# Broadcast of the softmax reciprocals issued one query block later, and the zero point of the int weights taken off by column sums instead of on the weights

## The reference

```
xn   = layernorm(x) * ln_scale + ln_bias
xg   = concat([16 global tokens, xn])                    # T = 2048 tokens + G = 16
Q, K, V = xg @ Wq.T, xg @ Wk.T, xg @ Wv.T                # 16 heads of 128
S    = Q K^T / sqrt(128) + mask                          # band of 256 keys, and the 16 global keys
attn = softmax(S) @ V
x1   = layernorm(x + (attn @ Wo.T + x))
gate = silu(x1 @ ((wq_gate - 128) * s_gate[:, None]).T)  # wq_* are int32 in 0..255, 5632 x 2048
up   = x1 @ ((wq_up - 128) * s_up[:, None]).T
y    = (gate * up) @ ((wq_down - 128) * s_down[:, None]).T
out  = layernorm(x1 + y)
```

## Time and profile before

| | us |
|---|---|
| median of 3 runs (lowest, highest) | 5631.65 (5619.04, 5742.77) |
| the profiled execution, its time | 5661.84 |
| its span on the slowest core, core 7 | 5660.3 |
| spans of the eight cores | 5595.5 to 5660.3 |
| PE busy | 3669.3 (65%) |
| DVE busy | 1381.9 (24%) |
| ACT busy | 930.2 (16%) |

### The profile page before, as it was taken

How to read it: one execution, slowest core, us unless ns; L and a number is a source line. 1 busy time by engine, 2 the same in 40 slices (tenths; PEclk the granted TensorE clock), 3 DMA queues, 4 the chain that set the end, 5 groups by cost and what they waited for, 6 DMA issues and landing times.

```text
span 5660.3 us, 46164 instructions; the slowest of 8 cores (5595.5 to 5660.3 us)
## 1 busy us (share of the span) xinstructions
PE 3669.3 (65%) x15128; PEld 1440.1 (25%) x15128; DVE 1381.9 (24%) x2076; ACT 930.2 (16%) x1175; POOL 302.8 (5%) x577
## 2 busy tenths in 40 slices
PE   2386686777677656170799985555129999755550
PEld 1132231232222112030344432222004444322220
DVE  6523323333322321324222210000241222000003
ACT  0001101111111110000233331111003333211110
POOL 0000000000000000000000001111000000111110
PEclk9977778888788778685799999998659999999895
DMA  2200100110110116433344433333334444233323
GB/s 81 67 10 14 35 11 13 28 19 13 29 19 8 17 30 117 134 89 144 80 75 76 80 56 51 40 50 62 98 126 78 75 75 75 45 52 52 62 34 150
DMA packets 210620, 335.31 MB, mean 59 GB/s; under 512 B 112452, under 2 KB 157509, under 8 KB 196565
## 3 DMA queue, kind: packets, MB, share of 16 engines
q0 software_dynamic: 82400, 180.46, 20.0%
q1 hardware_dynamic: 127990, 151.90, 8.2%
HBM read 458.20 MB, written 54.53 MB: 91 GB/s over the span
## 4 chain that ended last, share of the span: by engine, by line
PE 56%; DMA 17%; DVE 15%; issue 7%; ACT 3%; DVEq 1%; ACTq 0%; another core or an unknown queue 0%; SPq 0%; POOLq 0%; POOL 0%
PE p_gu L914 21%; DMA wdTt<-wd 9%; PE p_sc L452 5%; PE p_sc L500 4%; PE p_sc L464 4%; PE p_wo L699 4%; DVE rowBt L586 4%; PE p_gu L1024 4%; PE p_sc L546 2%; DVE statst L292 2%; DMA xrest<-x 2%; ACT wdTt L1006 2%; DMA r2tt<-r2sp 2%; PE p_srow L1162 2%; PE p_sc L549 2%
## 5 line engine op out<-in xcount | busy, mean ns | idle before, releaser
L1024 PE MATMUL p_gu<-wdTt,hmidt 128*128 128x512 bf16 x1408 | 401.8, 409 | 529.5 <-ACT wdTt L1006 501.0
L914 PE MATMUL p_gu<-xn2ht,wgTt 128*128 128x512 bf16 x2816 | 639.7, 380 | 31.1 <-ACT wuTt L890 28.8
L914 PE MATMUL p_gu<-xn2ht,wuTt 128*128 128x512 bf16 x2816 | 636.5, 379 | 0.0
L565 ACT ACTIVATE p_sbt<-p_sc 128x512 bf16<-128x512 f32 x352 | 208.8, 598 | 1446.0 <-PE p_sc L549 1446.0
L1006 ACT ACTIVATE wdTt<-wdTt 128x512 bf16<-128x512 bf16 x352 | 222.2, 631 | 1059.2 <-DMA wdTt<-wd 985.2
L699 PE MATMUL p_wo<-woTt,aott 128*128 128x512 bf16 x1024 | 229.1, 388 | 218.2 <-DMA aott<-aosp 177.5
L914 PEld LDWEIGHTS p_gu<-xn2ht,wgTt 128*128 128x128 bf16 x2816 | 275.4, 98 | 367.8 <-issue 40.7
L914 PEld LDWEIGHTS p_gu<-xn2ht,wuTt 128*128 128x128 bf16 x2816 | 275.5, 98 | 332.3
L1024 PEld LDWEIGHTS p_gu<-wdTt,hmidt 128*128 128x128 bf16 x1408 | 123.7, 101 | 784.7 <-issue 706.4
L883 ACT ACTIVATE wgTt<-wgTt 128x2048 bf16<-128x2048 bf16 x88 | 168.2, 1912 | 848.2 <-DMA wuTt<-wu 848.2
L600 PE MATMUL p_rbc<-rowHt,ones_rowt 1*128 1x512 bf16 x64 | 37.1, 580 | 408.1 <-DVE rowLt L593 408.1
(11 more groups left out here) (96 smaller groups left out, 3191.7 us busy)
## 6 DMA issues: line engine op xcount, KB each, us to landing
wgTt<-wg POOLq DMA_DIRECT2D x88, 512.0 KB, 5.1
wuTt<-wu POOLq DMA_DIRECT2D x88, 512.0 KB, 7.1
wdTt<-wd POOLq DMA_DIRECT2D x352, 128.0 KB, 2.9
r2tt<-r2sp SPq DMA_DIRECT2D x32, 1024.0 KB, 6.5
xtilet<-x SPq DMA_DIRECT2D x16, 1024.0 KB, 5.5
aott<-aosp SPq DMA_DIRECT2D x32, 512.0 KB, 4.2
woTt<-wo POOLq DMA_DIRECT2D x8, 2048.0 KB, 31.2
xrest<-x SPq DMA_DIRECT2D x16, 1024.0 KB, 6.9
```

The source lines that it names most:

```text
L565: return act.activation(p_sb[:, (i % 4) * 512:(i % 4 + 1) * 512], bank.p[:, :], AF.Exp)
L914: ins = t.matmul(bank.p[:, :], wsl[:, j * D + dc * 128:j * D + (dc + 1) * 128], xn2h[:, dc * 1024 + tc * 512:dc * 1024 + (tc + 1) * 512], ...
L1024: ins = t.matmul(pd_banks[ti].p[:, :], hmid[:, hb * 1024 + ti * 128:hb * 1024 + (ti + 1) * 128], wdT[:, j * 512:(j + 1) * 512], start=(hb ...
```

## The change

Two independent edits.

First, the tail of a query block is cut in two. The DVE row chain (`rowA` to `rowL`) stays where it was. The rest (the two matmuls L600 and L602, the copy L611, the multiply L619 and SP's store) is put into a list and written out only after the next block's last P V matmul, ahead of that block's own DVE row chain. The tail of a head's last block so comes after the first block of the next head, behind that head's Q and K matmuls.

Second, ACT no longer adds -128 to the weights: PE waits for the DMA itself. In its place PE sums `xn2h` over the contraction at the start of each pass (2 x 16 matmuls with one output row, into the one bank `b_cs`), DVE splits the row into `rowH` and `rowL`, and every bank of gate and up gets two more matmuls of 512 columns with one contraction row (`neg128` times `rowH`, `rowL`). Before down, `hmid` is summed in the same manner (2 x 44 matmuls), and after the 44th weight tile every one of the 8 banks gets two more matmuls, with `rowH` or `rowL` stationary and `neg128` moving. With this, PE waits for all 8 banks to be free before the first matmul of a column block; before, each matmul waited for its own bank.

The diff, cut to its core:

```diff
@@ attention, at the end of the P V matmuls of a block
                     emit_pv(h, q4, nk - 1, klist, hh, t_exp, t_pvmm, t_pv)
                     t_pv[(h, q4)] = s_pe.tok
+                    while pending_tail:
+                        pending_tail.pop(0)()
...
                     blk.vector(f)
                     t_rhl4 = s_dve.tok
-                    def f(t, h=h, q4=q4, t_rhl4=t_rhl4):
-                        wt(t, t_rhl4)
...
+                    def tail_fin(h=h, q4=q4, t_rhl4=t_rhl4):
+                        def f(t):
+                            wt(t, t_rhl4)
+                            wt(t, b_rb.freed)
+                            t.matmul(b_rb.p[:, :], ones_row[:, :], rowH[:, q4 * 512:(q4 + 1) * 512],
+                                     start=True, stop=False)
+                            ins = t.matmul(b_rb.p[:, :], ones_row[:, :], rowL[:, q4 * 512:(q4 + 1) * 512],
+                                           start=False, stop=True)
...
+                    pending_tail.append(tail_fin)
+
+        while pending_tail:
+            pending_tail.pop(0)()
         barrier()
@@ feed-forward, at the start of a pass
-            t_cshl = t_xn2
+            t_csev = {}
+            for tc in range(2):
+                def f(t, p=p, tc=tc, t_xn2=t_xn2):
+                    wt(t, t_xn2)
...
+                    wt(t, b_cs.freed)
+                    for dc in range(ND):
+                        ins = t.matmul(b_cs.p[0:1, :], ones_col[:, :],
+                                       xn2h[:, dc * 1024 + tc * 512:dc * 1024 + (tc + 1) * 512],
+                                       start=(dc == 0), stop=(dc == ND - 1))
...
@@ loads of gate and up
-                def fs(act, hb=hb, j=j, wgT=wgT, _t_ld=_t_ld, _t_pw=_t_pw,
...
-                    return act.activation(wgT[:, j * D:(j + 1) * D], wgT[:, j * D:(j + 1) * D],
-                                          AF.Copy, bias=-128.0)
...
+                t_wgld[hb] = s_wg[j].tok
@@ matmuls of gate and up
                             for dc in range(ND):
-                                ins = t.matmul(bank.p[:, :],
...
+                            t.matmul(bank.p[:, :], neg128[:, 0:128],
+                                     rowH[:, tc * 512:(tc + 1) * 512], start=False, stop=False)
+                            ins = t.matmul(bank.p[:, :], neg128[:, 0:128],
+                                           rowL[:, tc * 512:(tc + 1) * 512], start=False, stop=True)
@@ between gate/up and down
-            t_hcshl = t_hmid_all
+            for tc in range(2):
+                def f(t, p=p, tc=tc, t_hmid_all=t_hmid_all):
+                    wt(t, t_hmid_all)
+                    wt(t, b_cs.freed)
+                    for hb in range(NHB):
+                        ins = t.matmul(b_cs.p[0:1, :], ones_col[:, :],
...
@@ down
                         if hb == 0:
                             wt(t, t_hcshl)
+                            for ti in range(8):
+                                wt(t, pd_banks[ti].freed)
                         for ti in range(8):
-                            if hb == 0:
-                                wt(t, pd_banks[ti].freed)
...
                         if hb == NHB - 1:
                             for ti in range(8):
-                                pd_banks[ti].used = (s_pe, s_pe.n)
+                                t.matmul(pd_banks[ti].p[:, :],
+                                         rowH[:, ti * 128:(ti + 1) * 128], neg128[:, :],
+                                         start=False, stop=False)
+                                ins = t.matmul(pd_banks[ti].p[:, :],
+                                               rowL[:, ti * 128:(ti + 1) * 128], neg128[:, :],
+                                               start=False, stop=True)
+                                pd_banks[ti].used = s_pe.inc(ins)
```

More of the change, by code:

```diff
@@ L959, in build_nc, with f @@
             pxs.close()
-            t_hcshl = t_hmid_all
+            t_hcs_ev = {}
+            for tc in range(2):
+                def f(t, p=p, tc=tc, t_hmid_all=t_hmid_all):
+                    wt(t, t_hmid_all)
+                    wt(t, b_cs.freed)
+                    for hb in range(NHB):
+                        ins = t.matmul(b_cs.p[0:1, :], ones_col[:, :],
+                                       hmid[:, hb * 1024 + tc * 512:hb * 1024 + (tc + 1) * 512],
+                                       start=(hb == 0), stop=(hb == NHB - 1))
+                    b_cs.used = s_pe.inc(ins)
+                blk.tensor(f)
+                def f(dve, p=p, tc=tc):
+                    wt(dve, b_cs.used)
+                    dve.wait_ge(s_dve.h, s_dve.n)
+                    b_cs.freed = s_dve.inc(dve.tensor_copy(rowA[:, tc * 512:(tc + 1) * 512],
+                                                           b_cs.p[0:1, :]))
+                blk.vector(f)
+                t_hcs_ev[tc] = s_dve.tok
+            def f(dve, p=p):
+                wt(dve, t_hcs_ev[1])
+                dve.wait_ge(s_dve.h, s_dve.n)
+                s_dve.inc(dve.tensor_copy(rowH[:, 0:1024], rowA[:, 0:1024]))
+                dve.wait_ge(s_dve.h, s_dve.n)
+                s_dve.inc(dve.tensor_tensor(rowC[:, 0:1024], rowA[:, 0:1024],
+                                            rowH[:, 0:1024], ALU.subtract))
+                dve.wait_ge(s_dve.h, s_dve.n)
+                s_dve.inc(dve.tensor_copy(rowL[:, 0:1024], rowC[:, 0:1024]))
+            blk.vector(f)
+            t_hcshl = s_dve.tok
             b_s2 = [Bank(psa(p4p, "p_s20_%d" % p, [128, 512])),
@@ L1015, in build_nc, with f @@
                     j = hb % 2
+                    def f(pool, p=p, e4=e4, hb=hb, j=j):
+                        prev = t_dpe.get((p, e4, hb - 2)) or t_dpe.get((p, e4 - 1, NHB - 2 + hb)) \
+                            or t_dpe.get((p - 1, 3, NHB - 2 + hb))
+                        wt(pool, prev)
+                        if e4 == 0 and hb < 2:
+                            wt(pool, t_gu[(p, NHB - 1)])
+                            wt(pool, t_hmid[(p, NHB - 1, 1)])
+                            if p > 0:
+                                wt(pool, t_outst[(p - 1, 7)])
+                        s_wd[j].inc(pool.dma_start(out=wdT[:, j * 512:(j + 1) * 512],
+                                                   in_=wd_in[e4, hb * 128:(hb + 1) * 128, :]), 16)
+                    blk.gpsimd(f)
+                    t_wdld[(e4, hb)] = s_wd[j].tok
                     def f(t, p=p, e4=e4, hb=hb, j=j):
```

161 lines of the change are left out of this document (57 added, 104 removed).

## The result

The changed kernel is faster: the ratio of its time to that of the kernel before is 0.9412, 95% interval 0.9373 to 0.9451. The forecast was 5290 us, 0.939 of the time before. In most executions of either kernel the cores of one or both dies were granted a lower clock and the time was longer, so the ratios and the single times in this document are of executions without that (for the changed kernel 5287.04, 5300.87 and 5314.54 us, the first of them profiled). The median over eight executions of every kind is 5528.9 us (5287.04 to 5776.14); that of the kernel before is 5743.41 over ten, not the 5631.65 of the first three. The forecast was for a median, and 5528.9 lies above its range of 5190 to 5400 us.

What follows compares the result with a forecast made beforehand. PE was taken to bound the kernel, with large waits in down (501.0 us) and attention (408.1 us). Terms -496 + 215 + 4 + 40 - 129 + 21 = -345 from the 5631.65 median gave 5290 us, range 5190 to 5400.

Steps and rivals of the forecast that it cites:

- The sum of -345: Whole kernel: all forecast terms added, -496 + 215 + 4 + 40 - 129 + 21 = -345 us.
- Attention, -496: Attention: deferring the two matmuls saves 31.0 us a head over 16 heads, -496 us.
- t0: Attention: start of a block's last row-sum matmul (L1157 before); next first P V forecast 3.74 us later, 9.81 before.
- 6.33: Attention: forecast time in us from a full block's first P V to its last row sum.
- rival A: Attention gives back half: clock stays low between 1.2 us stalls, or unseen DVE step; time 5540 to 5630; chance 0.05.
- 17.53: Attention: time in us of a full block before the change; forecast 10.07 after.
- The wait at P V: Attention: new PE wait for DVE's `rowA` at a block's first P V, about 1.2 us, some 48 times.
- Gate and up, +215: Gate and up: 704 added matmuls cost 152 us, switches between 128 contraction rows and one 63 more.
- Rival B: Gate and up: one-row matmuls cost far more than 0.09 us a switch; kernel slower from 0.58; chance 0.02.
- Start of down, +20 a pass: Before down: sums of `hmid`, row work and waiting take 26.6 us instead of 6.47 idle; +40 in all.
- Down, -129 + 21: Down: load's turn 5.76 us instead of 6.53, -129 us; column-block transitions +20 and last blocks +1.
- Rival C: Dense stages: granted clock falls to 0.81 after the change, costing 300 us; time 5590; chance 0.03.

## Why the prediction was right and wrong

- **The time itself.** The failed step is "the forecast is for a median, so 5631.65 - 345". The median of three executions was taken for that of the kernel, and nothing was set down for its moving with more of them. Over ten it is 5743.41, and the changed kernel's over eight is 5528.9: outside the range, and 214 us below the one before, not 345. The sum of -345 itself fits the two profiled executions (5631.7 and 5285.5 us on core 0, 346 apart), and its 0.939 the measured 0.9412. But it fits by luck: two of its terms were wrong by about 100 us in opposite directions.
- **Attention, -496: right in mechanism, 95 us too large.** The first P V came at t0 + 3.63 against 3.74 worked out, the end of a head took 0.84 us instead of 1.05, `rowL` was ready, and `wqkT` never late. The step that failed is "6.33", the time from the first P V to the last row sum, taken from a stretch at full clock. PE stops for `rowA` in 47 of the 48 full blocks of core 0. After 39 of these stops the matmuls went on at half clock and it was 7.6 to 9.1 us; after the other 8 it was 6.32, the forecast's own number within 0.01. Three of the 8 are those of head 12, of which this is the first:

```profile
1399.31 0.37 PE L1173 MATMUL p_srow<-p_gt,ones_colt 16*1 16x512 bf16 x1
...
1402.94 0.38 PE L1176 MATMUL p_pv<-p_sbt,v4t 128*128 128x512 bf16 x1 [1.76 <-DVE rowAt L583]
...
1409.27 0.37 PE L1173 MATMUL p_srow<-p_gt,ones_colt 16*1 16x512 bf16 x1
```

   The mean block is 11.41 us and not 10.07, 64 us over the 48. The forecast had this as rival A and gave it 0.05 on the ground that PE in down stops for 2.85 us and still runs at full clock. That one turn was not the rule. In the same trace, on core 7, 24 of the 97 stops over 2.5 us in down are followed by matmuls at half clock; the earlier trace rows shows it after a longer one (4 matmuls in 1.87), and so does this one of the usual length:

```profile
3386.14 1.86 PE L1024 MATMUL p_gu<-wdTt,hmidt 128*128 128x512 bf16 x4 [2.83 <-ACT wdTt L1006]
```

   The experiment with the tail further forward shows that with a stop of 0.67 us in its place the half clock is gone. A second, smaller part: the 17.53 us a block before came from head 2 of core 7; the mean of the 48 on core 0 is 17.11, so 20 us of the gain were never there to be had.
- **The wait at P V was called 1.2 us and was 1.76.** The forecast took the difference of the two paths, 3.74 less 2.54; but PE stands idle from the end of the second score pair on, also while the exp that either path waits for is made. It was the stop and not the difference that had to be held against the clock.
- **Gate and up, +215: right.** 352 x (4.09 - 3.46) = 222 us, and the bounds and the choice of the row L1160 to L1162 for the switch held. Rival B (0.58 us a switch) is excluded by the 0.10 and 0.09 measured.
- **Start of down, +20 a pass: right.** 27.5 us against some 6.9 before.
- **Down, -129 + 21: 106 us too small a gain.** The failed step is the turn: "the load's turn loses ACT's 0.77". Over the eight column blocks of core 0, each from the end of its first weight tile to the end of its 44th (21.5 turns), the turns took 1194.3 us before and 972.2 after, 6.94 and 5.65 us each. A turn lost 1.29 us and not 0.77, 222 us in all and not 129. The 5.65 is close to the forecast's 5.76; it is the turn before that was read too short, from one of 6.53 in the earlier trace rows. Of the 222 us, 174 are PE's stops before a weight tile (478.1 to 304.3), and 51 are matmuls that no longer run at half clock: the eight matmuls of a tile took longer than the 1.51 us of full clock in 62 of 344 tiles before and in 24 after. The turn in the earlier trace rows had none of these. Why the stops alone shrank by 1.0 us a turn, and not by 0.77, is not shown. The transitions were nearly right: the six of core 0 take 96.1 us against 81.0, 15 us more for the +20 of the forecast.
- **Rival C (a clock of 0.81 after the change):** not in the profiled execution; gate and up and the first V projection ran at 1.00 on core 0 (2340 to 3000 us and 303 to 358 us).

## What to carry to other kernels

A wait that is moved off PE's path is worth more than its length if its end leaves PE without a stop, and less if a shorter stop stays: here moving the tail once more was worth 112 us. On core 0 the stop ahead of the first P V shrank from 1.75 to 0.69 us in the mean, 51 us over 48 blocks, while the half clock that had followed it was 71 us, the larger part (some 10 us went back elsewhere). So the deferred work belongs inside the next block where its result is ready, and not at its end. Where a chain of buffer free, DMA and in-place work holds an engine, ask first for more buffers; removing the last link gained 1.3 us of a 6.9 us turn, two more buffers took nearly the whole wait. And work on an idle engine should not be traded for work on the one that bounds: gate and up lost 216 us that way, while the same arithmetic on ACT was free.

## What had not been expected of the hardware

- The same stop of PE can leave the clock up or bring it down. In attention 39 of 47 stops of about 1.76 us were followed by matmuls at half clock (1.2 GHz), from the first P V on or one matmul later and for a part of the block; after the other 8 all matmuls of the block ran at full clock. With the stops shortened to 0.69 us the granted clock of the stretch was 1.00. In down, 24 of 97 stops over 2.5 us were followed by half clock. What else PE did around the stops differs, and these runs don't settle which part of it decides.
- Matmuls with one contraction row take the same 0.22 us for 512 columns as those with 128; only the change between the two costs, 0.10 us going in and 0.09 coming out. The 88 sums with one output row ran at 0.22 us each too (44 in 9.66 us), with no cost between them.
- More buffers for `wdT` in the kernel before gained more (560 us) than PE had waited for it (501). The listed waits leave out what hangs on each stop: 0.16 us up to the modelled end of the matmul before it, 38 us in all, and the half clock behind some of them, 43 us.
